# Turning and adding the partial sums of capsule routing in one product with stacked identities

## The chip, the cores and the metric

One core of one Trainium2 chip runs the whole program. The metric is the device time of one execution in microseconds (us); for the kernel before it is 13064.68 us, the median of three runs (13056.39 to 13068.2).

## The reference

The input is 16 images of 32 channels and 64x64 pixels. Two layers are added to it. The first, the only one that the change touches, is capsule routing over 3x3 patches: 4 input capsules of 8 channels vote for 4 output capsules of 8 channels, and three rounds weigh the votes.

```python
priors = jnp.einsum('nfdhwij,ofijud->nhwofiju', patches, weight)
logits = jnp.zeros_like(priors)
for r in range(3):
    probs = softmax(logits, axis=-3)
    out = jnp.sum(probs * priors, axis=-2, keepdims=True)
    if r != 2:
        out = squash(out)
        logits = logits + jnp.sum(priors * out, axis=-1, keepdims=True)
out = squash(out)
```

`squash(s)` is s·n²/((1+n²)·sqrt(n²+1e-12)) with n the length of a capsule's vector. The second layer is chunked attention with an MLP over the same patches, folded back. All of it is float32 at the borders.

## The kernel before, in words

The program has five phases with barriers between them: a norm, routing, a norm, attention, the fold. Only the routing phase changes.

**Tiling.** A pass handles half an image; there are 32 passes. A half has four lanes of 512 pixels. All 128 partitions hold 4 input capsules x 32 channels. A lane meets 9 taps (the 3x3 positions), and each tap is one tile of 128x512.

**Slots.** The work of a pass is laid out in 16 slots, in a loop whose body holds two passes. Slots 0 to 3 and 8 to 11 are voting slots (lane 0 to 3, rounds 0 and 1), slots 4 to 7 and 12 to 15 are summing slots. In a slot TensorE (`make`) writes nine tap tiles into four PSUM tiles `r_pg` in turn: in a voting slot with two bfloat16 products a tap (L582, L583), in a summing slot with four float32 transposes of 128x128 a tap (L587, out of `r_spread`). Each tile is multiplied by a shifted window of the image: seven taps on VectorE (L849), two on GpSimd (L524), for which ScalarE first copies the tile to SBUF (L790). TensorE then reduces the nine product tiles over channels (`batch`): L629 and L632 are taps in eights of instructions, L621 and L618 are tap 8. In a summing slot the result `r_ps` holds four partial sums of the lane: each 32 partitions of the 128 hold the sum over some of the taps.

**The order inside a slot** is written out by hand. TensorE: the first three taps; a light part C; tap 8 and then taps 4 to 7 of the slot before (this last group of eight products is called the mark of a slot below); a second light part C; four more taps; the light part A; the last two taps; taps 0 to 3 of this slot. VectorE: the product of the first tap; light part B; four products; light part A, with the last two products filled in between its steps. A tile of `r_pg` is written again only when the product four taps back has been read, and a batch waits for its products.

**Lights.** Beside the tap work each slot has small steps on a lane that was finished before. A squash light goes as follows. ScalarE copies `r_ps` to `r_sums` (L733). Part A on TensorE turns it with four float32 transposes of 128x128 (L663) into the PSUM tile `r_pt`: pixels are then on partitions, and the 512 columns are four blocks of pixels x four partial sums x 32 channels. VectorE adds the four partial sums with one tensor_reduce (L866), writing 128 columns to `r_cap`, then squares (L871), sums to lengths (L873), and computes 1+n² (L875) and its reciprocal (L878, L881); ScalarE computes the inverse root (L745, L748). Part B on VectorE scales (L908, L913) and in round 1 adds to the vote (L921). ScalarE and GpSimd split the vote in three bfloat16 parts (L762, L763, L547, L765, L549), and part C on TensorE turns them back (L668), or turns the output (L674). The squash lights of round 1 have their part A in slots 5 to 8, those of round 2 in slots 13 to 15 and slot 0 of the next pass. Slot 13 has also the round-0 light of the next pass, whose sums come from a uniform product over the image (L647) and which VectorE takes with a copy (L863). Slots 1 to 4 and 9 to 12 have softmax lights (L680, L888, L893).

All of the small constants are loaded by SyncE at the start of the phase, and TensorE and VectorE wait for them on the semaphore `fixed`.

Of the kernel before, what the change touches and what calls it, by code (L numbers as in the profile page):

```python
# [17 lines left out]
ALU = mybir.AluOpType  # L18
ACT = mybir.ActivationFunctionType
EXP_LN = "natural_log_exp_and_others"  # L20
AX_X = mybir.AxisListType.X

C = 32
# [10 lines left out]
LANES = 4  # L34
CHUNK = 512
CROWS = CHUNK // IMG
BLK = CHUNK // 128
# [291 lines left out]
def routing_phase(nc, ctx, sems, halves, routed, w_sum, w_vote, w_uniform, consts):  # L329
# [5 lines left out]
    def sb(n, shape, dt=F32):  # L335
        return ctx.enter_context(nc.sbuf_tensor(f"r_{n}", shape, dt))
# [12 lines left out]
    ident = sb("ident", [128, 128])  # L349
    ident_b = sb("ident_b", [128, 128], BF16)  # L350
    pick = sb("pick", [128, 2, C])
    eps = sb("eps", [128, 1])
    prod = sb("prod", [128, TAPS, CHUNK])

# [136 lines left out]

    @block.sync
    def _(sp):
        for to, src in ((ws[:, :, :], w_sum), (wu[:, :, :], w_uniform), (ident[:, :], consts["ident"]), (pick[:, :, :], consts["pick"])):
            sp.dma_start(to, src).then_inc(fixed, 16)
        for k in range(4):
            sp.dma_start(wv_f[C * k:C * k + C, :], w_vote).then_inc(fixed, 16)
        with sp.Fori(0, passes // 2) as i:
            for h in range(2):
                n = 2 * i + h  # L500

                sp.wait_ge(products.sem, products.at(n, -n_dve * SLOTS))
                sp.wait_ge(pooled.sem, pooled.at(n, -len(POOLED) * SLOTS))
                for k in range(CAPS):
                    to = win[C * k:C * k + C, h, :, :].rearrange("p a b -> p (a b)")
                    sp.dma_start(to, halves[n, :, :]).then_inc(loaded[h].sem, 16)
                image = halves[n, :, :].rearrange("c (a b) -> c a b", b=PAD)
                for j in range(3):
                    to = wsh[C * j:C * j + C, h, :].rearrange("p (a b) -> p a b", b=IMG)
                    sp.dma_start(to, image[:, :, j:j + IMG]).then_inc(loaded[h].sem, 16)  # L510
# [43 lines left out]
    @block.tensor  # L554
    def _(pe):
        pe.sem_inc(reduced.sem, reduced.base)
        pe.wait_ge(fixed, 16 * 8)
        pe.wait_ge(prepared, 1)

        def make(n, s, pos):  # L560
# [90 lines left out]
        def light(p, x, which):  # L651
            d, kind, r, lane, part = x
            n = p.to(d).n

            before = reader_before(x, which)
            if before:
                free, k = before
                pe.wait_ge(free.sem, free.at(p.n, k))
            if kind == "squash" and part == "A":
                own = sums[:, 1 + lane % 2 if r else 0, :]  # L660
                pe.wait_ge(sum_copied[r].sem, sum_copied[r].at(n, lane + 1))
                for b in range(BLK):
                    last = pe.transpose(pt[:, 128 * b:128 * b + 128], own[:, 128 * b:128 * b + 128], ident[:, :])  # L663
                last.then_inc(sum_turned[r].sem, 1)
            elif kind == "squash" and r < 2:
                pe.wait_ge(part2[r].sem, part2[r].at(n, lane + 1 if r else 1))
                for b in range(BLK):
                    last = pe.transpose(pt_b[:, 128 * b:128 * b + 128],  # L668
                                        parts[:, lane, b, :, :].rearrange("p a b -> p (a b)"), ident_b[:, :])
                last.then_inc(parts_turned[r].sem, 1)  # L670
            elif kind == "squash":
                pe.wait_ge(squashed[2].sem, squashed[2].at(n, lane + 1))
                for b in range(BLK):
                    last = pe.transpose(pt[0:C, 128 * b:128 * b + 128], sq[:, 1, lane, C * b:C * b + C], ident[:, :])  # L674
                last.then_inc(out_turned.sem, 1)
            else:
                pe.wait_ge(logit_copied[r].sem, logit_copied[r].at(n, lane + 1))
                pe.wait_ge(logit9_copied[r].sem, logit9_copied[r].at(n, lane + 1))
                for b in range(BLK):
                    pe.transpose(pt[:, 128 * b:128 * b + 128], logit[:, lane % 2, 128 * b:128 * b + 128], ident[:, :])  # L680
                last = pe.transpose(pl9[:, 0:128], logit9[:, lane % 2, :], ident[:, :])
                last.then_inc(logit_turned[r].sem, 1)
# [139 lines left out]
    def _(dve):  # L822
# [8 lines left out]
            dve.wait_ge(chain, step[0])  # L831

        dve.wait_ge(fixed, 16 * 8)
        link(nc.vector.tensor_copy(wv_0[:, :], wv_f[:, :]))
        link(nc.vector.tensor_tensor(wv_r[:, :], wv_f[:, :], wv_0[:, :], ALU.subtract))
        link(nc.vector.tensor_copy(wv_1[:, :], wv_r[:, :]))
# [16 lines left out]
        def light_a(n, kind, r, lane, fill):  # L854

            k = lane + 1
            if kind == "squash":
                own = int(r > 0)
                c, s2, nm, fc = (tile[:, own, lanes_of(r, lane), :].rearrange("p l x -> p (l x)")
                                 for tile in (cap, sq, norm, fac))  # L860
                dve.wait_ge(sum_turned[r].sem, sum_turned[r].at(n, k))
                if r == 0:
                    last = nc.vector.tensor_copy(cap[:, 0, :, :].rearrange("p l (b c) -> p l b c", c=C),  # L863
                                                 pt[:, :].rearrange("p (b l c) -> p l b c", b=BLK, c=C))
                else:
                    last = nc.vector.tensor_reduce(c.rearrange("p (b c) -> p b c", c=C),  # L866
                                                   pt[:, :].rearrange("p (b g c) -> p b c g", b=BLK, c=C), AX_X, ALU.add)
                last.then_inc(summed[r].sem, 1)
                fill()
                dve.wait_ge(summed[r].sem, summed[r].at(n, k))  # L870
                nc.vector.tensor_tensor(s2, c, c, ALU.mult).then_inc(squared[r].sem, 1)  # L871
                dve.wait_ge(squared[r].sem, squared[r].at(n, k))
                nc.vector.tensor_reduce(nm, s2.rearrange("p (k u) -> p k u", u=CLEN), AX_X, ALU.add).then_inc(normed[r].sem, 1)  # L873
                dve.wait_ge(normed[r].sem, normed[r].at(n, k))
                nc.vector.tensor_scalar(fc, nm, 1.0, None, ALU.add).then_inc(plus1[r].sem, 1)  # L875
                fill()
                dve.wait_ge(plus1[r].sem, plus1[r].at(n, k))
                nc.vector.reciprocal(fc, fc).then_inc(recip[r].sem, 1)  # L878
                fill()
                dve.wait_ge(recip[r].sem, recip[r].at(n, k))  # L880
                nc.vector.tensor_tensor(fc, fc, nm, ALU.mult).then_inc(ratio[r].sem, 1)  # L881
                return
            dve.wait_ge(logit_turned[r].sem, logit_turned[r].at(n, k))

            pieces = ((pt[:, :].rearrange("p (k x) -> p k x", x=16), 0, 32),
                      (pl9[:, 0:128].rearrange("p (k x) -> p k x", x=C)[:, :, 0:16], 32, 36))
            for src, a, b in pieces:
                nc.vector.tensor_reduce(top[:, lane, 4 * a:4 * b].rearrange("p (k f) -> p k f", f=CAPS),  # L888
                                        src.rearrange("p k (o f) -> p k f o", o=CAPS), AX_X, ALU.max).then_inc(maxed[r].sem, 1)
            fill()  # L890
            dve.wait_ge(maxed[r].sem, maxed[r].at(n, 2 * k))
            for src, a, b in pieces:
                last = nc.vector.tensor_tensor(  # L893
                    low[:, lane, 16 * a:16 * b].rearrange("p (k o f) -> p k o f", o=CAPS, f=CAPS),
                    src.rearrange("p k (o f) -> p k o f", o=CAPS),
                    over_capsules(top[:, lane, 4 * a:4 * b], b - a), ALU.subtract)
            last.then_inc(shifted[r].sem, 1)
# [921 lines left out]
        finish(Pass(samples - 1, 1, samples // 2 - 1), 1)  # L1819

def program(nc, x, w_sum, w_vote, w_uniform, w_r, w_qkv, w_p, w_1, b_1, w_2, ident, pick, pairs,
            sample, count, sel, result):

    batch = x.shape[0]
# [13 lines left out]
    def phase(body, *args):  # L1839

        sems = []
        with ExitStack() as ctx:
            body(nc, ctx, sems, *args)
        nc.clear_and_free_semaphores(sems)
        nc.all_engine_barrier()

    phase(norm_phase, "n1", rows, None, dict(pairs=pairs), first)
    phase(routing_phase, first, routed, w_sum, w_vote, w_uniform, dict(ident=ident, pick=pick))
    phase(norm_phase, "n2", rows, routed, dict(pairs=pairs, sample=sample, count=count), second, layered, total)
    phase(attention_phase, second, layered, mixed, moments, w_r, w_qkv, w_p, dict(ident=ident))  # L1850
    phase(fold_phase, mixed, moments, total, result.rearrange("b c h w -> (b c) (h w)"), w_1, w_2, b_1,
# [3 lines left out]
def lay_out(inputs):  # L1855
# [14 lines left out]
    for p in range(128):  # L1870
# [8 lines left out]
        w_qkv=inputs["L1_conv_Wqkv"].T, w_p=w_p.reshape(QUADS, 128, 3, 3 * C),  # L1879
        w_1=inputs["L1_conv_W1"].reshape(HID, C, 3, 3).transpose(3, 1, 2, 0).reshape(3 * C, 3, HID),  # L1880
        b_1=inputs["L1_conv_b1"].reshape(HID, 1), w_2=w_2.reshape(3 * C, 3, 3 * C),
        ident=np.eye(128, dtype=f), pick=pick,
        pairs=np.kron(np.eye(64, dtype=f), np.full((2, 2), 0.5, f)),
        sample=np.kron(np.eye(4, dtype=f), np.full((C, C), 1 / (PIX * DIM), f)),
        count=np.outer(times, times).reshape(1, PIX),
# [19 lines left out]
```

## Time and profile before

| | |
|---|---|
| Median of three runs | 13064.68 us (13056.39 to 13068.2) |
| Profiled execution | 13060.79 us, span 13059.0 us |
| Mean granted TensorE clock | 0.982 |
| TensorE matmul busy | 12449.1 us, 95% |
| TensorE weight load busy | 5276.3 us, 40% |
| VectorE busy | 9722.8 us, 74% |
| ScalarE busy | 7866.5 us, 60% |
| GpSimd busy | 2684.0 us, 21% |

The span is that of the core from its first to its last instruction. Matmuls are pipelined, and their ends are modelled, so a busy share of TensorE overstates how full the engine is: the distance between the starts of successive instructions tells more. PE is TensorE's matmul, PEld its weight load, DVE VectorE, ACT ScalarE, POOL GpSimd. Idle time in brackets is that of the engine in front of the row, with what ended it.

### The profile page before, as it was taken

The page shows a single profiled execution, that of the slowest core. Times are in us where ns is not written, and L with a number is a line of the kernel's source. Part 1 is how long each engine was busy: PE and PEld are TensorE (multiplying, and loading weights), DVE is VectorE, ACT ScalarE, POOL GpSimd, SP SyncE. Part 2 cuts the span into 40 slices and gives each one's busy share as a digit, 9 for nine tenths or more (in the row PEclk, how much of TensorE's full clock was granted, in tenths as well). Part 3 has the DMA queues.
Part 4 walks back from the last instruction along what each step waited for, and adds up shares of the span by engine and source line. Part 5 has one row for each costly group of instructions (what it writes and reads, how often), then busy time and mean ns, then how long its engine had stood idle before and what let it go on. Part 6 is the DMA issues. An engine that isn't in the chain of part 4 may idle for free. (4 is left out here: it accounts for less than half of the span.)

```text
span 13059.0 us, 258656 instructions
## 1 busy us (share of the span) xinstructions
PE 12449.1 (95%) x76092; PEld 5276.3 (40%) x76348; DVE 9722.8 (74%) x18034; ACT 7866.5 (60%) x14774; POOL 2684.0 (21%) x2692
## 2 busy tenths in 40 slices
PE   6999999999996499999999999999999999999899
PEld 3555555555553133333333333333333333333233
DVE  7888888888887577777777777777777777777311
ACT  4666666666665166666666666666666666666411
POOL 3454444544443000000000000000000000000143
PEclk9999999999998699999999999999999999999999
DMA  3101011010112523223222232332322323223255
GB/s 77 22 15 22 17 20 22 15 22 15 22 21 55 132 64 75 66 66 73 66 70 69 67 72 66 73 70 64 75 66 67 72 66 71 68 69 72 64 124 109
DMA packets 853225, 771.45 MB, mean 59 GB/s; under 512 B 587076, under 2 KB 621348, under 8 KB 840740
## 3 DMA queue, kind: packets, MB, share of 16 engines
q1 hardware_dynamic: 850468, 747.29, 25.4%
q8 instruction: 703, 11.52, 0.4%
q10 hardware_dynamic: 1536, 8.39, 0.3%
q14 instruction: 518, 4.24, 0.1%
HBM read 510.50 MB, written 244.96 MB: 58 GB/s over the span
## 5 line engine op out<-in xcount | busy, mean ns | idle before, releaser
L1503 DVE TENSOR_REDUCE a_big<-a_mp 128x1 f32<-128x512 f32 x8192 | 5222.3, 685 | 1816.0 <-PE a_mp L1337 1797.7
L1423 ACT ACTIVATE a_ex<-a_sc 128x512 f32<-128x512 f32 x8192 | 4426.4, 601 | 1937.6 <-PE a_sc L1325 1932.6
L1337 PE MATMUL a_mp<-a_ks,a_qs 108*128 108x512 bf16 x8192 | 3131.1, 383 | 39.9 <-DMA a_ks<-qk_parts 25.1
L1325 PE MATMUL a_sc<-a_qs,a_ks 111*128 111x512 bf16 x8192 | 3124.5, 383 | 6.8 <-ACT a_ex L1423 4.5
L849 DVE TENSOR_TENSOR r_prod<-r_pg,r_win 128x512 f32<-128x512 f32 x3584 | 2319.4, 683 | 416.5 <-PE r_pg L583 227.9
L1351 PE MATMUL a_po<-a_ex,a_va 128*32 128x512 f32 x16384 | 2183.0, 605 | 2.1 <-ACT a_oc L1429 0.7
L1239 POOL TENSOR_TENSOR a_pieces<-a_left,a_pieces 128x512 bf16<-128x512 f32 x256 | 295.5, 1154 | 7319.5 <-ACT a_pieces L1409 7319.5
L1325 PEld LDWEIGHTS a_sc<-a_qs,a_ks 111*128 111x128 bf16 x8192 | 794.9, 97 | 2477.6 <-ACT a_ex L1423 1767.0
L524 POOL TENSOR_TENSOR r_prod<-r_temp,r_win 128x512 f32<-128x512 f32 x1024 | 1214.7, 1207 | 1298.3 <-PE r_pl L632 568.3
L587 PE MATMUL r_pg<-r_ident,r_spread 128*128 128x128 f32 x9216 | 1196.7, 278 | 113.3 <-DVE r_prod L849 94.5
L587 PEld LDWEIGHTS r_pg<-r_ident,r_spread 128*128 128x128 f32 x9216 | 1004.9, 142 | 573.0 <-DVE r_prod L849 275.1
L1337 PEld LDWEIGHTS a_mp<-a_ks,a_qs 108*128 108x128 bf16 x8192 | 803.2, 98 | 913.6 <-DVE a_big L1503 237.7
L807 ACT ACTIVATE r_spread<-r_low 128x2048 f32<-128x2048 f32 x512 | 952.1, 1916 | 0.0
L582 PE MATMUL r_pg<-r_stack,r_wv 96*128 96x512 bf16 x2304 | 882.3, 383 | 28.4 <-DVE r_prod L849 10.1
L583 PE MATMUL r_pg<-r_stack,r_wv 128*128 128x512 bf16 x2048 | 778.4, 380 | 0.0
L1269 PE MATMUL a_pm<-a_zw,a_wc 96*128 96x512 f32 x1536 | 711.1, 599 | 15.1 <-DVE a_left L1473 13.4
L1351 PEld LDWEIGHTS a_po<-a_ex,a_va 128*32 128x32 f32 x16384 | 322.5, 107 | 824.7 <-ACT a_ex L1423 702.6
L629 PE MATMUL r_ps<-r_prod,r_ws 128*32 128x512 f32 x4096 | 553.3, 613 | 22.8 <-DVE r_prod L849 15.6
L1808 DVE TENSOR_TENSOR f_u<-f_pw,f_three 96x512 f32<-96x512 f32 x128 | 87.9, 687 | 651.4 <-PE f_pw L1677 650.1
L790 ACT COPY r_temp<-r_pg 128x512 f32<-128x512 f32 x1024 | 544.1, 583 | 20.4 <-ACT r_out_t L775 20.4
L632 PE MATMUL r_pl<-r_prod,r_pick 128*32 128x512 f32 x4096 | 541.1, 600 | 5.3 <-DVE r_prod L849 0.3
L1723 ACT ACTIVATE f_hidden<-f_ph,f_coef 72x512 f32<-72x512 f32 x128 | 99.0, 773 | 652.2 <-PE f_ph L1667 652.2
(192 smaller groups left out, 11795.2 us busy)
## 6 DMA issues: line engine op xcount, KB each, us to landing
a_qs<-qk_parts SPq DMA_DIRECT2D x768, 144.0 KB
a_ks<-qk_parts SPq DMA_DIRECT2D x768, 144.0 KB
qk_parts<-a_pieces SPq DMA_DIRECT2D x128, 768.0 KB, 5.0
f_t<-mixed SPq DMA_DIRECT2D x48, 1536.0 KB, 16.7
a_tw<-second SPq DMA_DIRECT2D x512, 128.0 KB, 3.1
mixed<-a_t SPq DMA_DIRECT2D x256, 256.0 KB, 2.1
r_win<-first SPq DMA_DIRECT2D x128, 280.5 KB, 5.2
a_zw<-layered SPq DMA_DIRECT2D x192, 144.0 KB, 12.2
```

The costliest lines, as they stand in the source:

```text
L524: nc.gpsimd.tensor_tensor(prod[:, g, :].rearrange("p (a b) -> p a b", b=IMG), temp[:, rank, :].rearrange("p (a b) -> p a b", b=IMG), tap_a ...
L582: pe.matmul(bank[:, :], wv_0[0:96, w], stack[0:96, lane, :], start=True, stop=False)
L583: last = pe.matmul(bank[:, :], wv_12[:, w], stack[:, lane, :], start=False, stop=True)
L587: last = pe.transpose(bank[:, 128 * b:128 * b + 128], spread[:, lane, 16 * kk:16 * kk + 16, :].rearrange("p a b -> p (a b)"), ident[:, :])
L807: nc.scalar.activation(to[:, :, half, :], src[:, :, half].unsqueeze(3).to_broadcast([128, BLK, 64, CLEN]), ACT.Exp).then_inc(prob[r].sem, 1)
L849: nc.vector.tensor_tensor(prod[:, g, :].rearrange("p (a b) -> p a b", b=IMG), pg[use % RINGS][:, :].rearrange("p (a b) -> p a b", b=IMG), ...
L1269: last = pe.matmul(pm[:, :], wc[:, i, 128 * (k % WIDE):128 * (k % WIDE) + 128], zw[:, own.h, first:first + CHUNK], start=i == 0, stop=i == 2)
L1325: pe.matmul(sc[k % BANKS][:, :], ks[0:KROWS + NPART, p.h, head, 128 * kb:128 * kb + 128], qs[0:KROWS + NPART, p.h, head, CHUNK * qb:CHUNK ...
L1337: pe.matmul(mp[k % BANKS][:, :], qs[0:KROWS, p.h, head, 128 * q:128 * q + 128], ks[0:KROWS, p.h, head, CHUNK * half:CHUNK * half + CHUNK], ...
L1351: last = pe.matmul(po[32 * x:32 * x + 32, :], va[:, p.h, kb, QUAD * quad + x, :], ex[:, (QUAD * t + x) % RING, :], start=kb == 0, stop=kb ...
L1423: nc.scalar.activation(ex[:, k % RING, :], sc[k % BANKS][:, :], ACT.Exp, scale=scale).then_inc(exped.sem, 1)
L1503: nc.vector.tensor_reduce(big[:, x % 2, k // 2:k // 2 + 1], mp[k % BANKS][:, :], AX_X, ALU.max).then_inc(maxed.sem, 1)
```

## The change

In rounds 1 and 2 the four transposes of part A become four products. Each takes the same 128x128 block of `r_sums` as its stationary operand, and as its moving operand, in place of the 128x128 identity, a new constant `gather` of 128x32: four 32x32 identities on top of one another. One such product turns the block and adds its four partial sums, so the result has 32 columns for a block and 128 for the lane. VectorE's tensor_reduce over 512 columns becomes a tensor_copy of 128 columns from PSUM to SBUF. Round 0 is unchanged. The constant is one more load at the start of the phase, so the waits on `fixed` go from 8 to 9 loads.

```diff
+    gather = sb("gather", [128, C])
 ...
-        for to, src in ((ws[:, :, :], w_sum), (wu[:, :, :], w_uniform), (ident[:, :], consts["ident"]), (pick[:, :, :], consts["pick"])):
+        for to, src in ((ws[:, :, :], w_sum), (wu[:, :, :], w_uniform), (ident[:, :], consts["ident"]), (pick[:, :, :], consts["pick"]), (gather[:, :], consts["gather"])):
 ...
-        pe.wait_ge(fixed, 16 * 8)
+        pe.wait_ge(fixed, 16 * 9)
 ...
                 for b in range(BLK):
-                    last = pe.transpose(pt[:, 128 * b:128 * b + 128], own[:, 128 * b:128 * b + 128], ident[:, :])
+                    if r == 0:
+                        last = pe.transpose(pt[:, 128 * b:128 * b + 128], own[:, 128 * b:128 * b + 128], ident[:, :])
+                    else:
+                        last = pe.matmul(pt[:, C * b:C * b + C], own[:, 128 * b:128 * b + 128], gather[:, :],
+                                         start=True, stop=True)
 ...
-        dve.wait_ge(fixed, 16 * 8)
+        dve.wait_ge(fixed, 16 * 9)
 ...
-                    last = nc.vector.tensor_reduce(c.rearrange("p (b c) -> p b c", c=C),
-                                                   pt[:, :].rearrange("p (b g c) -> p b c g", b=BLK, c=C), AX_X, ALU.add)
+                    last = nc.vector.tensor_copy(c, pt[:, 0:BLK * C])
 ...
+        ident=np.eye(128, dtype=f), pick=pick, gather=np.tile(np.eye(C, dtype=f), (LANES, 1)),
```

## Rows read from the trace of the kernel before

**Rows 1.** Busy by stretch (length, PE, PEld, DVE, ACT, POOL, clock, DMA): routing; rows 4.

```profile
326.00:3600.00 3274.00, 3128.63 (x24793) 1668.18 (x24992) 2853.01 (x5705) 2130.08 (x3683) 1635.45 (x1708) 0.99 0.11 19
...
12285.00:12287.00 2.00, 1.22 (x8) 1.12 (x8) 0.53 (x3) 0.00 (x0) 0.00 (x0) 0.50 1.01 221
```

**Rows 2.** Groups of instructions, VectorE: busy us, mean ns, idle before, releaser.

```profile
L866 DVE TENSOR_REDUCE r_cap<-r_pt 128x128 f32<-128x512 f32 x256 | 174.1, 680 | 68.6 <-PE r_pt L663 68.6
...
L893 DVE TENSOR_TENSOR r_low<-r_pl,r_top 128x64 f32<-128x64 f32 x256 | 54.9, 214 | 0.0
...
L863 DVE COPY r_cap<-r_pt 128x512 f32<-128x512 f32 x32 | 22.0, 687 | 10.8 <-PE r_pt L663 10.8
```

**Rows 3.** Groups of instructions, TensorE: products and weight loads, float32.

```profile
L1305 PEld LDWEIGHTS a_pm<-a_on,a_wp 128*128 128x128 f32 x1024 | 194.2, 190 | 165.5 <-issue 124.5 <-DVE a_t L1496 2.4 <-DVE a_on L1485 1.1
L663 PE MATMUL r_pt<-r_ident,r_sums 128*128 128x128 f32 x1152 | 176.1, 275 | 2.0 <-ACT r_sums L733 1.2 <-ACT r_sums L730 0.8
...
L1310 PEld LDWEIGHTS a_pm<-a_on,a_wp 128*32 128x32 f32 x1024 | 26.9, 110 | 40.3 <-DVE a_t L1496 28.8 <-issue 0.7
```

**Rows 4.** Timeline, TensorE: start us, us, runs of one float32 product, two places.

```profile
5083.44 2.37 PE L1282 MATMUL a_pm<-a_wc,a_zw 96*128 96x144 f32 x18
...
12285.49 0.80 PEld L1655 LDWEIGHTS f_px<-f_ones,f_w 96*72 96x72 f32 x6 [22.94 <-issue]
```

**Rows 5.** Timeline, VectorE, slots 6 to 10 of one pass: start us, us.

```profile
1562.40 0.69 DVE L849 TENSOR_TENSOR r_prod<-r_pg,r_win 128x512 f32<-128x512 f32 x1
...
1564.60 1.16 DVE L921 TENSOR_TENSOR r_vote<-r_vote,r_sq 128x128 f32<-128x128 f32 x1
...
1580.17 2.48 DVE L849 TENSOR_TENSOR r_prod<-r_pg,r_win 128x512 f32<-128x512 f32 x4 [1.10 <-PE r_pg L583]
...
1587.07 2.48 DVE L849 TENSOR_TENSOR r_prod<-r_pg,r_win 128x512 f32<-128x512 f32 x4 [0.97 <-PE r_pg L583]
```

**Rows 6.** Timeline, TensorE, the same pass, slots 5 to 10; L629, L632: marks.

```profile
1539.82 1.04 PE L629 MATMUL r_ps<-r_prod,r_ws 128*32 128x512 f32 x8
...
1546.45 0.43 PE L621 MATMUL r_ps<-r_prod,r_ws 128*32 128x128 f32 x8
1546.69 1.04 PE L629 MATMUL r_ps<-r_prod,r_ws 128*32 128x512 f32 x8
...
1555.46 1.06 PE L629 MATMUL r_ps<-r_prod,r_ws 128*32 128x512 f32 x8
...
1558.26 0.60 PE L663 MATMUL r_pt<-r_ident,r_sums 128*128 128x128 f32 x4
...
1562.26 0.38 PE L668 MATMUL r_pt<-r_ident_b,r_parts 128*128 128x128 bf16 x4
1562.57 0.42 PE L621 MATMUL r_ps<-r_prod,r_ws 128*32 128x128 f32 x8
1563.14 1.07 PE L629 MATMUL r_ps<-r_prod,r_ws 128*32 128x512 f32 x8
...
1578.53 1.06 PE L632 MATMUL r_pl<-r_prod,r_pick 128*32 128x512 f32 x8
```

**Rows 7.** Timeline, GpSimd, the same pass: start us, us, idle before.

```profile
1553.62 0.43 POOL L549 TENSOR_TENSOR r_parts<-r_rest,r_parts 128x128 bf16<-128x128 f32 x1 [0.41 <-ACT r_parts L765]
...
1564.32 2.48 POOL L524 TENSOR_TENSOR r_prod<-r_temp,r_win 128x512 f32<-128x512 f32 x2 [3.96 <-PE r_ps L629]
```

**Rows 8.** Timeline, TensorE, slot 14: start us, us, idle before.

```profile
1616.09 1.25 PE L587 MATMUL r_pg<-r_ident,r_spread 128*128 128x128 f32 x8 [2.08 <-DVE r_prod L849]
...
1621.35 1.06 PE L629 MATMUL r_ps<-r_prod,r_ws 128*32 128x512 f32 x8 [0.75 <-DVE r_prod L849]
```

**Rows 9.** Timeline, VectorE, slots 14 to 0, two passes: start us, us, idle before.

```profile
1496.60 2.48 DVE L849 TENSOR_TENSOR r_prod<-r_pg,r_win 128x512 f32<-128x512 f32 x4 [0.91 <-PE r_pg L587]
...
1619.58 1.12 DVE L875 TENSOR_SCALAR r_fac<-r_norm 128x16 f32<-128x16 f32 x1
...
1630.67 2.48 DVE L849 TENSOR_TENSOR r_prod<-r_pg,r_win 128x512 f32<-128x512 f32 x4 [0.84 <-PE r_pg L583]
```

More of the change, by code:

```diff
@@ L1819, in _, with program @@
         finish(Pass(samples - 1, 1, samples // 2 - 1), 1)
-def program(nc, x, w_sum, w_vote, w_uniform, w_r, w_qkv, w_p, w_1, b_1, w_2, ident, pick, pairs,
+def program(nc, x, w_sum, w_vote, w_uniform, w_r, w_qkv, w_p, w_1, b_1, w_2, ident, pick, gather, pairs,
             sample, count, sel, result):
@@ L1847, in program @@
     phase(norm_phase, "n1", rows, None, dict(pairs=pairs), first)
-    phase(routing_phase, first, routed, w_sum, w_vote, w_uniform, dict(ident=ident, pick=pick))
+    phase(routing_phase, first, routed, w_sum, w_vote, w_uniform, dict(ident=ident, pick=pick, gather=gather))
     phase(norm_phase, "n2", rows, routed, dict(pairs=pairs, sample=sample, count=count), second, layered, total)
@@ L1881, in lay_out @@
         b_1=inputs["L1_conv_b1"].reshape(HID, 1), w_2=w_2.reshape(3 * C, 3, 3 * C),
-        ident=np.eye(128, dtype=f), pick=pick,
+        ident=np.eye(128, dtype=f), pick=pick, gather=np.tile(np.eye(C, dtype=f), (LANES, 1)),
         pairs=np.kron(np.eye(64, dtype=f), np.full((2, 2), 0.5, f)),
```

## The prediction

> **What bounds the kernel now.** I read the busy time by stretch first, because the change lies in routing alone. In its steady part of 3274 us TensorE's matmuls are busy for 3129 us and VectorE for 2853 us, at a granted clock of 0.99 [rows 1]. Neither is idle enough to be ignored, so the groups of instructions give the prices of the pieces, and the timeline of one pass shows which engine ends each slot. Marks are what to follow there: the eight products with which TensorE closes the slot before. Where VectorE starts its four products straight behind its own work, VectorE sets the slot; where there is idle time in front of them that TensorE ends, TensorE does.
>
> Two kinds of squash slot come out. In slots 6 to 8 VectorE runs without a gap. The last product that the mark of slot 7 needs ends at 1562.40 + 0.69 = 1563.09, and the mark comes at 1563.14 [rows 5, 6]: TensorE waited for VectorE. The marks stand 1563.14 − 1555.46 = 7.68 us apart. In the slots around them TensorE sets the pace: 0.97 and 1.10 us of idle before VectorE's four products in slots 10 and 11 [rows 5], 0.91 us in slot 15 and 0.84 us in slot 0 [rows 9].
>
> **The change, part by part.** *VectorE* loses a reduction of 680 ns, 256 times: 8 in each of 32 passes [rows 2]. The copy of 128 columns from PSUM doesn't stand in the trace. The nearest rows are the copy of 512 columns at 687 ns and an operation of 64 columns from PSUM at 214 ns; they give (687 − 214)/448 = 1.06 ns a column and 214 + 64 × 1.06 = 282 ns, between 214 and 687. I take 280, so 0.40 us less a light, 102 us in all if VectorE were the bound everywhere.
>
> *TensorE* had four transposes. A run of four lasts 0.60 us and one lasts 0.275, so they start (0.60 − 0.275)/3 = 0.108 us apart [rows 3, 6], and the four take 0.43 us. A float32 product that is no transpose is two instructions with a weight load each: a mark is four calls, one a tap, and its rows show x8 [rows 6]. So the new light has eight loads of 128 columns and eight products of 32. The price is in the load. A load of 128 columns lasts 190 ns, one of 32 lasts 110 [rows 3]: 0.83 ns a column, 107 ns for 128 at the higher clock level. Where products have one column only, loads set the pace: six of 72 columns take 0.80 us with about 0.24 for the first, at a granted clock of 0.50 [rows 1, 4], so 0.112 apart, 0.056 at full clock, 0.78 ns a column, 100 ns for 128. The loads run beside products: 18 products of 144 columns, with loads of 128, take 2.37 us [rows 4], at most 2.37/18 = 0.132 apart and about 0.123 with the last one's 0.28 us taken as 275 ns like L663's [rows 3], and 144 columns alone are 0.120 at the same 0.83 ns. So eight take 8 × 0.107 = 0.853, and about 0.03 more because the last product of 32 columns (27 ns at 0.120/144 a column) no longer covers the load behind it: 0.88 us. TensorE has D = 0.45 us more a light. The lower end of the price is 8 × 0.027 = 0.22 us, loads free, D = −0.21; the upper end is eight whole loads of 190 ns, 1.52 us, D = 1.08. I stay with the loads' pace, which the two places of rows 4 carry.
>
> The rule that speaks against the change is in the Trainium skill, "TensorE: Matmul & The Clock Gate", Part 3, The mechanism: a weight load overlaps running products only where the row groups differ, and here they are all the same. By it load and product add up, 8 × 0.134 = 1.07 us and D = 0.63; the 0.123 us above speaks against it, since load and stream would be 0.107 + 0.120 there.
>
> *Slots 5 to 8 (round 1).* I carry the marks forward. Slot 5 to slot 6 was 1546.69 − 1539.82 = 6.87 with TensorE never waiting [rows 6]; it becomes 7.32, mark at 1547.14. A slot with a part C costs 0.31 more (1562.26 to 1562.57), so TensorE alone would need 6.87 + 0.31 + 0.45 = 7.63 for the next. But part C waits for the split vote, done at 1553.62 + 0.43 = 1554.05, which is 7.36 behind the old mark and hangs on ScalarE's long exponentials, started by that mark [rows 7]. With 0.05 for the signal and 0.31 + 0.24 from part C to the mark [rows 6] the next mark is at 1547.14 + 7.36 + 0.60 = 1555.10 instead of 1555.46. Then 7.63 gives 1562.73 instead of 1563.14. Slot 8 is a voting slot; a softmax voting slot with a part C, paced by TensorE, takes 1587.07 − 1580.17 = 6.90 [rows 5]; a transpose fewer (0.11) and D make 7.24, mark at 1569.97. Slot 9 is then TensorE's at 6.90: 1576.87 instead of 1578.53. The gain is 1.66 us a pass. It rests on VectorE no longer being the bound. Its slot was 7.68 and has 0.40 less, 7.28, below 7.63. What it held beyond that was a stall: L921, 1.16 us, stands beside GpSimd's product, which started at 1564.32, released by the mark [rows 5, 7]. If VectorE gets there before the mark releases GpSimd, that stall goes too. VectorE is late no more; next is TensorE itself.
>
> *Slots 13 to 0 (round 2).* In slot 13 the light is waited for by VectorE: its start moves by between D − 0.40 = 0.05 and D; I take 0.23. In slot 14 TensorE idles 2.08 us right behind the light [rows 8], which hides D. There the mark waits 0.75 us for VectorE, and VectorE's L875 has lasted 1.12 us [rows 8, 9]: with 0.40 less it runs before the GpSimd work that holds it. So this mark gains those 0.75 and the 0.18 by which a run like L621 (0.42 to 0.43) outlasts its 0.24 to the mark, less the 0.23: −0.70, in one pass of two. In the other the four products of slot 15 wait for TensorE [0.91, rows 9], nothing is gained, and 0.23 is lost. Slots 15 and 0 are TensorE's: 2 × 0.45 lost. Over two passes −0.70 + 0.23 + 1.80 = 1.33, so 0.66 a pass.
>
> *The new constant* is one more small load in a queue; at most 1 us, once.
>
> Sum: −1.66 + 0.66 = −1.00 a pass, × 32 = −32 us, and with the load −31. From the profiled 13060.79 that is 13030; the profiled execution stands 4 below the median of the runs, so I name 13064.7 − 31.5 = 13033. The sum has a slope: each 0.1 us of D costs 3 × 0.1 in slots 5 to 8 (slot 6 has cover) and as much in the others, 6 × 0.1 × 32 = 19 us. It is even at D = 0.62.
>
> **The rivals.** *A, TensorE pays and VectorE's time isn't wanted.* Loads don't overlap. Slots become longer by D where TensorE is the bound, and from D = 0.78 in slot 6 too. With D = 0.63 the pass has −1.00 + 6 × 0.18 = +0.08, 13068; with D = 1.08 it has −1.00 + 6 × 0.33 + 7 × 0.30 = +3.08, 99 us, 13163. It is slower by more than 26 us from D = 0.75 on. For: the load, 190 ns, is seven times its product. Against: the 0.123 us. Chance 0.10.
>
> *B, no change.* VectorE stays behind in slots 6 to 9, because GpSimd's product, released by the mark, still meets L921, and the two stalls at slots 9 and 14 stay. Then slots 5 to 9 give 0.40 instead of 1.66, slot 14 only 0.40 − 0.23 = 0.17 instead of 0.70, and the pass has −0.40 + (−0.17 + 0.23 + 1.80)/2 = +0.53, 17 us: 13082. With half of the 1.66 it would be +0.10, 13068. For: the collision came in nearly every slot of this kind. Chance 0.30.
>
> *C, more than forecast.* D is hidden in slots 15 and 0 too (TensorE's order has waits there that the view credits to nothing), or ScalarE's chain in slot 6 is shorter. Then −1.66 − (0.70 − 0.23)/2 = −1.90 a pass, 61 us: 13004. For: little. Chance 0.15.
>
> *D, the change doesn't do what it says*: the copy is held up by GpSimd as L921 is and costs as much as the reduction. Against: L863 and L866, which read PSUM, average 687 and 680 ns over all their runs [rows 2]; that holds them to one price. Nothing would be saved, and slots 15 and 0 would cost 0.90 a pass, 29 us: 13094; chance 0.03.
>
> **How the numbers follow.** The forecast has 0.42, with its own range 13015 to 13050. No change can be told here within 0.2%, 26 us, so 13039 is the border of faster. Of the forecast two thirds lie below, 0.28; with a tenth of B and all of C that is 0.28 + 0.03 + 0.15 = 0.46. Slower by more than 26 us (above 13091): most of A, some of B and D, 0.11. Within: 0.43. The range reaches from C's side to B's upper end and a part of A: 12995 to 13088.
>
> **What would show it.** L663 as x8 in a run of about 0.95 us in rounds 1 and 2, loads 0.107 apart at 190 ns each. The copy at 280 ns. Marks of slots 6 to 8 about 7.6 apart, now with idle time of VectorE, L921 near 290 ns instead of 1160. Slots 15 and 0 longer by 0.45. The forecast is wrong if the run of eight lasts over 1.2 us, if L921 keeps 1.16 us, or if the marks keep 7.68.

## The result, and the profile after

| | before | after |
|---|---|---|
| Median of 20 runs | 13064.01 us (13056.23 to 13068.75) | 13082.74 us (13070.99 to 13097.76) |
| Profiled execution | 13060.79 us | 13070.99 us |
| Span, mean granted TensorE clock | 13059.0 us, 0.982 | 13069.2 us, 0.980 |

The ratio is 1.0014, with an interval of 1.0008 to 1.0021: the kernel is 19 us slower. That is inside the range of the prediction and within its 0.2%, but the forecast, 31 us faster, had the sign wrong.

The busy times moved as they should. First the page's part 1 of after, then the same stretch of routing as [rows 1] (length, PE, PEld, DVE, ACT, POOL, clock, DMA).

```profile
PE 12518.9 (96%) x77372; PEld 5425.0 (42%) x77372; DVE 9482.7 (73%) x18034; ACT 7854.6 (60%) x14774; POOL 2677.2 (20%) x2692
```

```profile
326.00:3600.00 3274.00, 3175.35 (x25735) 1784.20 (x25724) 2649.85 (x5683) 2112.18 (x3667) 1625.04 (x1703) 0.99 0.11 19
```

VectorE has 240 us less to do, TensorE 70 us more matmul and 149 us more weight load. The groups of after, by shape (busy us, mean ns, idle before, releaser), give the prices:

```profile
L667 PEld LDWEIGHTS r_pt<-r_gather,r_sums 128*128 128x128 f32 x2048 | 253.5, 191 | 36.8 <-issue 26.0 <-ACT r_out_t L780 1.5
L667 PE MATMUL r_pt<-r_gather,r_sums 128*128 128x32 f32 x2048 | 253.0, 267 | 1.2 <-ACT r_sums L738 1.2
L871 DVE COPY r_cap<-r_pt 128x128 f32<-128x128 f32 x256 | 71.6, 280 | 82.2 <-PE r_pt L667 82.2
L925 DVE TENSOR_TENSOR r_vote<-r_vote,r_sq 128x128 f32<-128x128 f32 x128 | 37.3, 292 | 4.4
L879 DVE TENSOR_SCALAR r_fac<-r_norm 128x16 f32<-128x16 f32 x256 | 44.6, 174 | 8.9
L917 DVE TENSOR_TENSOR r_sq<-r_cap,r_fac 128x128 f32<-128x128 f32 x256 | 103.7, 405 | 8.7
```

The copy costs 280 ns, as priced. The vote (L925, before L921) fell from 149.3 us of busy time in the kernel before to 37.3. All of its executions, before and then after (duration ns min/median/max, first and last start):

```profile
L921 DVE TENSOR_TENSOR r_vote<-r_vote,r_sq x128: 1152/1159/1310, 158.1 to 4098.6; 128x128 f32<-128x128 f32 x128
```

```profile
L925 DVE TENSOR_TENSOR r_vote<-r_vote,r_sq x128: 291/292/293, 159.0 to 4106.5; 128x128 f32<-128x128 f32 x128
```

In the kernel before all 128 begin while a GpSimd operation runs, in the kernel after none does. L879 and L917 (before L875 and L913) fell from means of 290 and 548 ns to 174 and 405 in the same way: of L913's 256 executions 68 begin beside a running GpSimd operation and take 1.25 us, and the other 188 take 0.29; of L917's 31 do. So of VectorE's 240 us some 102 are the copies' (256 × 0.40), and nearly all of the rest is time lost beside GpSimd.

TensorE in slots 5 to 10 of a pass (start us, us, runs of one instruction); L630 and L633 are the marks:

```profile
1416.40 1.04 PE L630 MATMUL r_ps<-r_prod,r_ws 128*32 128x512 f32 x8
...
1419.17 0.98 PE L667 MATMUL r_pt<-r_gather,r_sums 128*128 128x32 f32 x8
...
1423.68 1.04 PE L630 MATMUL r_ps<-r_prod,r_ws 128*32 128x512 f32 x8
...
1431.18 0.38 PE L673 MATMUL r_pt<-r_ident_b,r_parts 128*128 128x128 bf16 x4 [0.38 <-POOL r_parts L550]
...
1431.74 1.04 PE L630 MATMUL r_ps<-r_prod,r_ws 128*32 128x512 f32 x8
...
1439.20 1.04 PE L630 MATMUL r_ps<-r_prod,r_ws 128*32 128x512 f32 x8
...
1446.58 1.04 PE L633 MATMUL r_pl<-r_prod,r_pick 128*32 128x512 f32 x8
...
1453.69 1.04 PE L633 MATMUL r_pl<-r_prod,r_pick 128*32 128x512 f32 x8
```

The marks are 7.28, 8.06, 7.46, 7.38 and 7.11 apart, where [rows 6] has 6.87, 8.77, 7.68 and, for the last two together, 15.39. VectorE and GpSimd in the same pass:

```profile
1432.06 0.29 DVE L925 TENSOR_TENSOR r_vote<-r_vote,r_sq 128x128 f32<-128x128 f32 x1
1433.40 2.48 DVE L854 TENSOR_TENSOR r_prod<-r_pg,r_win 128x512 f32<-128x512 f32 x4 [1.05 <-PE r_pg L588]
...
1440.82 2.48 DVE L854 TENSOR_TENSOR r_prod<-r_pg,r_win 128x512 f32<-128x512 f32 x4 [0.47 <-PE r_pg L584]
```

```profile
1432.89 2.35 POOL L525 TENSOR_TENSOR r_prod<-r_temp,r_win 128x512 f32<-128x512 f32 x2 [1.85 <-PE r_ps L630]
...
1440.35 2.33 POOL L525 TENSOR_TENSOR r_prod<-r_temp,r_win 128x512 f32<-128x512 f32 x2 [3.89 <-PE r_ps L630]
```

VectorE's vote ends at 1432.35, and only then, at 1432.89, does GpSimd start, released by the mark. VectorE now waits for TensorE (1.05 and 0.47 us in brackets); in the pass of [rows 5] its products of slots 6 to 8 follow its other work without a gap.

Below, a table of marks says how much later or earlier each mark follows the one before than it does in the kernel before, as means in us over the passes of the loop. The row of a slot is the time from its mark to the next one. The forecast's column has its own steps.

| Mark of slot | forecast | after |
|---|---|---|
| 5 to 6 | +0.45 | +0.41 |
| 6 to 7 | −0.81 | −0.71 |
| 7 to 8, to 9, to 10 | −0.05, −1.25 for the other two | −0.21, −0.30, −0.61 |
| slot 13, with its light | +0.23 | +0.25 |
| slot 14, in the pass of [rows 8] | −0.93 (−0.70 with slot 13's) | +0.25 |
| slot 14, in the other pass | 0 | +0.09 |
| slots 15 and 0, inside the loop's body | +0.45, +0.45 | +0.39, +0.37 |
| slot 15, at the end of the loop's body | +0.45 | +2.15 |
| slot 0 behind it | +0.45 | +0.02 |

Slots 5 to 9 (round 1) gained 1.42 us a pass, near the forecast's 1.66. Two lines are far off: slot 14, and the place where TensorE's loop ends, once in two passes. At the loop's end the trace of after reads so (TensorE's timeline):

```profile
1498.88 0.98 PE L667 MATMUL r_pt<-r_gather,r_sums 128*128 128x32 f32 x8
1499.69 1.07 PE L588 MATMUL r_pg<-r_ident,r_spread 128*128 128x128 f32 x8
1500.70 1.06 PE L630 MATMUL r_ps<-r_prod,r_ws 128*32 128x512 f32 x8
1503.79 0.51 PE L583 MATMUL r_pg<-r_stack,r_wv 96*128 96x512 bf16 x1 [2.03 <-issue]
1504.09 0.63 PE L584 MATMUL r_pg<-r_stack,r_wv 128*128 128x512 bf16 x1
```

TensorE is idle for 2.03 us, and no engine ends the wait: "issue" stands for time in which it waited for nothing that the profile shows. The loop's own line at this place (duration ns min/median/max, first and last start):

```profile
L317 PEldq COMPARE_BRANCH  x1: 3592/3592/3592, 1499.8 to 1499.8; - x1
```

The branch back to the loop's start took 3.6 us. TensorE worked off what was already queued and then had nothing to run. In that same stretch the DMA view shows one packet, of the queue that carries instructions:

```profile
DMA  0000000000080000000000000000000000000000
...
DMA packets 1, 0.02 MB, mean 5 GB/s; under 512 B 0, under 2 KB 0, under 8 KB 0
...
q8 instruction: 1, 0.02, 2.1%
```

It stands in the twelfth of 40 slices of 1499.80 to 1503.40, so about 1.0 us after the branch began, and the branch ends 2.6 us behind it. Over all 15 executions of the branch (the last one isn't taken, 80 ns), before, then after:

```profile
L317 PEldq COMPARE_BRANCH  x15: 80/836/2447, 488.0 to 4024.6; - x15
```

```profile
L317 PEldq COMPARE_BRANCH  x15: 80/3333/3793, 485.4 to 4032.7; - x15
```

The 14 taken ones have a mean of 1.30 us before and 3.32 us after. The same branch takes 44 to 90 ns on the other engines in both. The Trainium skill, "Runtime: NRT & Kernel Launch", section Instruction fetch mechanics, describes this: instructions are streamed in order in 16 KiB blocks, "Branching breaks sequential prefetch", and a taken branch whose target isn't in the window stalls until the target is fetched. The trace agrees in so far as a packet of 0.02 MB of the instruction queue stands inside the branch and TensorE runs dry; in these two kernels the taken branch lasts 0.35 to 3.8 us.

### The profile page after: what moved, and what is told of

It is laid out like the page before. It is cut to its first block and busy times, and to the rows that moved or that the text cites. A ratio compares the mean times of both kernels' runs of the same rounds, so it can differ in the third digit from the quotient of the medians.

```text
span 13069.2 us, 260961 instructions
## 1 busy us (share of the span) xinstructions
PE 12518.9 (96%) x77372; PEld 5425.0 (42%) x77372; DVE 9482.7 (73%) x18034; ACT 7854.6 (60%) x14774; POOL 2677.2 (20%) x2692
## 5 line engine op out<-in xcount | busy, mean ns | idle before, releaser
L584 PE MATMUL r_pg<-r_stack,r_wv 128*128 128x512 bf16 x2304 | 877.3, 381 | 0.0
L630 PE MATMUL r_ps<-r_prod,r_ws 128*32 128x512 f32 x4096 | 560.6, 620 | 1.0 <-DVE r_prod L854 1.0
L633 PE MATMUL r_pl<-r_prod,r_pick 128*32 128x512 f32 x4096 | 539.4, 598 | 0.0
```

What stands on the lines that cost most here:

```text
L584: last = pe.matmul(bank[:, :], wv_12[:, w], stack[:, lane, :], start=False, stop=True)
```

## The experiments

Each was timed in three or five rounds against the kernel before on the same chip; the chips differ between groups of experiments, so each time is compared with the kernel before beside it. After each stands the ratio with its interval. The marks are again means against the kernel before. The theory at the start was that the parts do what was foretold and that what is lost comes at the loop's end and in slot 14; rivals were that VectorE's saving or TensorE's cost was mis-sized.

**One part at a time.** The kernel before with the copy alone (e1: it copies 128 columns of the transposes' result and leaves the sum of the four parts out), and the kernel after with the reduction of 512 columns kept (e2: it adds columns that the product didn't write).

```diff
 # e1, on the kernel before
-  last = nc.vector.tensor_reduce(c..., pt[:, :]..., AX_X, ALU.add)
+  last = nc.vector.tensor_copy(c, pt[:, 0:BLK * C])
 # e2, on the kernel after: the reverse
```

> The four transposes stay; VectorE copies the first 128 columns instead of reducing 512, so one partial sum of one block is taken where the sum of four belongs. TensorE's instructions are those of before, to the last one. Theory 1 (the slots behave as forecast, and what made the change slower is TensorE's taken branch at the end of the loop, 0.84 us in the median before and 3.33 after): the branch stays near 0.8 us, the marks of slots 6 to 9 come 0.5 to 0.8 us earlier each, slot 14 gains too, together about 3 us a pass: 12970 to 12990. Theory 2 (VectorE's time is not wanted, TensorE is the bound everywhere): within 25 us of before.

e1: 13001.97 us (12998.52 to 13007.31), 0.9958 (0.9945 to 0.9972), 56 us faster, and less than the 12970 to 12990 expected. The vote keeps its stall (in 122 of 128 executions):

```profile
L866 DVE COPY r_cap<-r_pt 128x128 f32<-128x128 f32 x256 | 71.8, 280 | 68.6 <-PE r_pt L663 68.6
...
L920 DVE TENSOR_TENSOR r_vote<-r_vote,r_sq 128x128 f32<-128x128 f32 x128 | 143.3, 1119 | 4.4
```

Round 1 gains 1.21 us a pass, by 0.30, 0.44, 0.40 and 0.07 in slots 6 to 9: VectorE is the bound, and three of its slots are shorter by about its 0.40. The branch, expected near 0.8, has a median of 1.92 us, though every instruction of TensorE is that of the kernel before.

> The eight products are there, and VectorE still runs its reduction over 512 columns, of which 384 are old, so what it adds up is not the sum. Theory 1: +0.41 us in the mark of slot 5, little in slots 6 to 9 where VectorE sets the pace, +0.4 in slots 15 and 0, +0.45 or more in slot 13, about 1.5 us a pass = 48 us, and on top the branch at 3.3 us, some 18 us more: 13125 to 13135. Theory 2 (no effect of the branch): the same without the 18, about 13110, and the branch near 0.8 us.

e2: 13079.86 us (13072.61 to 13085.86), 1.0017 (1.0008 to 1.0026). A miss, and the most telling one: VectorE still pays 683 ns a light, and yet round 1 has the marks of the kernel after to 0.01 us (+0.41, −0.71, −0.21, −0.30, −0.60), and the vote's stall is gone:

```profile
L871 DVE TENSOR_REDUCE r_cap<-r_pt 128x128 f32<-128x512 f32 x256 | 174.7, 683 | 82.1 <-PE r_pt L667 82.1
...
L926 DVE TENSOR_TENSOR r_vote<-r_vote,r_sq 128x128 f32<-128x128 f32 x128 | 37.4, 292 | 4.4
```

So in round 1 VectorE's 0.40 us is not what was gained. TensorE being later was. In the whole kernel, too, e2 and the kernel after can't be told apart (1.0017 and 1.0014 of the kernel before).

**That, by itself.** The kernel before with the four transposes of round 1 done twice: pure extra work, nothing of the change (f1).

```diff
-  for b in range(BLK):
+  for b in [*range(BLK)] * (2 if r == 1 else 1):
```

> The kernel before, with one addition: in round 1 TensorE does the four transposes of part A twice over, the second time onto the first. It is work for nothing, 0.43 us and 8 instructions a light; VectorE's reduction stays. Theory 1 (round 1 gains because a later TensorE releases GpSimd's product later, so that VectorE's addition to the vote no longer meets it, and the shorter VectorE operation has no part in it): the marks of slots 5 to 9 are those of the changed kernel (+0.41, -0.71, -0.21, -0.30, -0.61 us), the kernel is faster by about 39 us, 13020 to 13030. Theory 2 (round 1 gains by VectorE's 0.40 us): +0.41 in slot 5 and no gain behind it, 13065 to 13080.

13020.73 us (13016.28 to 13025.2), 0.9972 (0.9961 to 0.9982): useless work makes the kernel 36 us faster. Marks of round 1: +0.44, −0.72, −0.19, −0.23, −0.60. The branch is short here as well (0.35 us), but at the loop's end that changes little: slot 15 is 0.50 shorter there and slot 0 behind it 0.62 longer. The reduction is whole, the vote free, and the light's row is now a run of eight, as in after:

```profile
L866 DVE TENSOR_REDUCE r_cap<-r_pt 128x128 f32<-128x512 f32 x256 | 174.0, 680 | 68.7 <-PE r_pt L663 68.7
...
L921 DVE TENSOR_TENSOR r_vote<-r_vote,r_sq 128x128 f32<-128x128 f32 x128 | 37.3, 292 | 4.4
```

```profile
1421.42 1.04 PE L663 MATMUL r_pt<-r_ident,r_sums 128*128 128x128 f32 x8
```

**The two rounds apart.** The kernel after with the change in round 1 alone (e3) and in round 2 alone (e4); the condition stands in both places, TensorE's and VectorE's.

```diff
-  if r == 0:
+  if r != 1:      # e4: if r != 2
```

> Only round 1 (slots 5 to 8) has the new product and copy, round 2 stays as before. By the marks of the changed kernel round 1 gains 1.45 us a pass, 46 us. TensorE's loop body is longer by 64 instructions instead of 128. Theory 1, if the branch grows with the length of the body: between 0 and 18 us of the gain is lost, 13018 to 13036, with the branch between 0.8 and 3.3 us in the median. If the branch depends on the length in steps it is at one of the two ends. Theory 2 (the changed kernel's loss is the light's own price, in both rounds): 13070 to 13075, half of the loss.

> Only round 2 (slots 13 to 15 and slot 0) has the new product and copy. By the marks of the changed kernel, without the wait at the loop's end, it loses about 1.05 us a pass, 34 us. Theory 1: that and the branch, 13098 to 13116. Theory 2 (half of the loss each): 13070 to 13075. The sum of this one's and the round-1 kernel's differences should give the changed kernel's +19 us if the rounds don't meet; a rest between them is the branch's.

e3: 13019.43 us (13012.63 to 13022.4), 0.9970 (0.9959 to 0.9981). e4: 13059.5 us (13054.7 to 13065.69), 1.0002 (0.9993 to 1.0011). Apart they are worth −39 and +1 us, together +19: 56 us are in neither part. e3 came as expected in time; e4 is 39 us below its lower forecast of 13098 and 11 below the other theory's 13070. The ratios of e3 and f1 can't be told apart: in round 1 the change is worth what doing the transposes twice is worth. In both e3 and e4 the branch takes 0.35 us, shorter than in the kernel before; here e3:

```profile
L317 PEldq COMPARE_BRANCH  x15: 80/349/391, 486.1 to 3984.5; - x15
```

e4 shows slot 14 in two passes. The same two runs, TensorE:

```profile
2123.26 1.97 PE L588 MATMUL r_pg<-r_ident,r_spread 128*128 128x128 f32 x8 [1.71 <-DVE r_prod L854]
2125.16 1.68 PE L630 MATMUL r_ps<-r_prod,r_ws 128*32 128x512 f32 x8
...
2376.02 1.25 PE L588 MATMUL r_pg<-r_ident,r_spread 128*128 128x128 f32 x8 [1.71 <-DVE r_prod L854]
2377.22 1.06 PE L630 MATMUL r_ps<-r_prod,r_ws 128*32 128x512 f32 x8
```

```profile
2123.00:2127.00 4.00, 3.74 (x18) 2.00 (x19) 3.93 (x10) 3.22 (x7) 1.49 (x2) 0.57 0.00 0
2376.00:2380.00 4.00, 3.98 (x32) 2.64 (x32) 3.93 (x10) 3.03 (x7) 1.72 (x2) 1.00 0.00 0
```

After the same idle time of 1.71 us the clock is granted at 0.57 on average over 4 us in one pass, which is the lower level (1.2 of 2.4 GHz) in most of it, and at 1.00 in the other: the two runs take 3.58 us instead of 2.26. So slot 14 gains where the clock holds and gains nothing where it falls. By the marks, of what e3 and e4 together lack of the kernel after's loss, 2.4 us in two passes is at the loop's end and 1.2 is in slot 14.

**The loop's end without the change.** The kernel before with 32 small bfloat16 transposes in slot 14 of one lane, where TensorE idles 2 us. With their weight loads the loop's body grows by 128 instructions, as it does with the change (f2).

```diff
+  if r == 2 and lane == 1:
+      for _ in range(32):
+          pe.transpose(pt_b[:, 0:128], ident_b[:, :], ident_b[:, :])
   pe.wait_ge(sum_copied[r].sem, sum_copied[r].at(n, lane + 1))
```

> The kernel before, with 32 bfloat16 transposes of an identity (64 instructions) in front of part A in slot 14 of each pass, where TensorE idles 2.1 us: the loop body has 128 instructions more, as in the changed kernel, and nothing of the change. Theory 1: the branch at the end of the loop rises from 1.3 us in the mean to about 3.3, slot 15 to 0 is longer by 1.5 us in one pass of two, 13075 to 13090. Theory 2 (the branch's wait comes from what the change does in time, not from the length of the body): branch as before, 13050 to 13065.

13085.39 us (13077.65 to 13090.9), 1.0021 (1.0011 to 1.003), 26 us slower. The mark at the loop's end comes 2.43 us later, where 1.5 was expected. The branch:

```profile
L317 PEldq COMPARE_BRANCH  x15: 80/3533/3774, 487.5 to 4047.8; - x15
```

**The change, with its code moved.** The kernel after, with N waits on a semaphore that has its value already, ahead of routing's first product. They do nothing but move TensorE's later code; the trace shows N/2 instructions more.

```diff
   pe.wait_ge(fixed, 16 * 9)
   pe.wait_ge(prepared, 1)
+  for _ in range(N):          # N = 64, 128, 192, 256
+      pe.wait_ge(fixed, 16 * 9)
```

> The changed kernel, with 64 waits more in TensorE's program in front of its first product of routing, each on what has already come, at a place where TensorE waits for data anyway. The loop itself is the same, only 64 instructions further back in memory. Theory 1 (the taken branch of TensorE's loop waits for the 16 KB piece of its program that holds the loop's start, and when that is fetched hangs on where the loop's ends lie in such pieces): the branch leaves 3.3 us, towards 0.35 or up to the 2.4 of before, and with 0.35 the kernel is faster than the changed one by 25 to 55 us, because the idle times that lower TensorE's clock go as well: 13030 to 13060. Theory 2 (the wait is the price of a longer loop, wherever it lies): 3.3 us, 13083.

> As the kernel with 64 waits, with 128. A piece of 16 KB holds 256 instructions of 64 bytes if they are of one length, so 64, 128 and 192 are quarters of a turn. Theory 1: the three differ from one another, at least one has the branch near 0.35 us and at least one above 2 us. Theory 2: all three have 3.3 us and 13083.

> As the kernel with 64 waits, with 192. Theory 1: see there; the one of the three with the shortest branch runs at 13030 to 13060. Theory 2: 3.3 us and 13083.

> The changed kernel with 256 waits more (the trace counted 32 instructions for 64 waits, so 128 here) in front of TensorE's first product of routing. So far the branch was 3.32, 2.76, 2.00 and 1.19 us in the mean with 0, 32, 64 and 96 instructions. Theory 1 (the place of the loop's ends in the pieces that are fetched): the row goes on to 0.35 to 0.6 us, the attention loop's branch back to about 0.36, and the kernel runs at 13035 to 13050; TensorE's low-clock stretches in slot 14 stay, so it doesn't reach the forecast. Theory 2 (chance): the branch is anywhere between 0.35 and 3.5.

| N | time, us | ratio (interval) | branch, median ns |
|---|---|---|---|
| 64 | 13118.43 | 1.0045 (1.0029 to 1.006) | 2770 |
| 128 | 13051.52 | 0.9996 (0.9986 to 1.0005) | 2235 |
| 192 | 13046.77 | 0.9991 (0.9981 to 1.0) | 752 |
| 256 | 13033.73 (13032.13 to 13042.92) | 0.9981 (0.9972 to 0.9991) | 349 |

```profile
L317 PEldq COMPARE_BRANCH  x15: 80/349/387, 489.4 to 4001.7; - x15
```

The last has all the work of the kernel after and 256 idle waits, and is 25 us faster than the kernel before beside it, where after is 19 slower. With 64, 128 and 192 waits the branch had been expected near 0.35 us at least once; only N = 256 has it. N = 64 was a miss with a reason: its routing is faster than after's, but the code of the attention phase moved too, and that phase's loop, 30 executions, now pays. Before, then N = 64:

```profile
L986 PEldq COMPARE_BRANCH  x30: 88/357/393, 5020.1 to 12051.1; - x30
```

```profile
L992 PEldq COMPARE_BRANCH  x30: 87/3008/3692, 5022.5 to 12116.1; - x30
```

From the first to the last branch this phase lasts 7093.6 us instead of 7031.0, and nothing of the change is in it.

**Which lights are worth it.** Round 1 and one lane of round 2 (f4, the condition `r == 1 or r == 2 and lane == 1`), or two (g3, lanes 1 and 3).

> The new product and copy in round 1 and in lanes 1 and 3 of round 2 (slots 14 and 0); lanes 0 and 2 (slots 13 and 15) as before. The body is longer by 96 instructions. Slot 14 had 10.80 us instead of 11.60 where the clock held, slot 0 lost 0.37 and won back a collision of VectorE with GpSimd in slot 0 that costs 1.24 us in the next mark. Theory 1: with a short branch -1.45 - 0.6 - 0.4 us a pass, 12980 to 13000; with a branch of 2 to 3 us some 20 more, 13000 to 13020. Theory 2 (round 2's light costs what it costs in each slot): no better than round 1 alone, 13020 or more.

> The new product and copy in round 1 and in lane 1 of round 2 (slot 14), body longer by 80 instructions. Theory 1: round 1 alone (-39 us) and the gain of slot 14, 0.8 us a pass where the clock holds, about 0.4 in the mean, 13 us: 13000 to 13015 with a short branch. The collision in slot 0 stays, so it is behind the kernel with lanes 1 and 3 unless that one's branch is longer. Theory 2: 13020.

g3: 13013.28 us (13006.9 to 13018.3), 0.9964 (0.995 to 0.9978); it missed its 13000. The collision in slot 0 that it was to win back stays: the mark behind the loop's end comes 0.56 us later. Where the branch is short, VectorE's light in slot 0 meets GpSimd's product, and the slot takes 8.69 us instead of 7.45 (kernel before), 1.24 more. f4: 13003.53 us (13002.2 to 13012.02), 0.9960 (0.9946 to 0.9973), 55 us faster than the kernel before. It has the lowest median of those that compute the whole, but its interval overlaps those of g3, e3 and f1, so that the added lane pays is not shown. Its branches are short as well (mean 0.35 us), which must be counted to it: the same work at another address need not give this.

## Why the prediction was wrong

*Prices.* They held: copy 280 ns, weight loads 191 ns; the eight products occupy TensorE for 0.81 us (1498.88 to 1499.69 above) for a forecast 0.88, and D, forecast at 0.45, shows as +0.41 in slot 5. Rival A is dead: the eight are 0.10 us apart, where load and product in turn would need 0.134, so the loads overlap, as the 0.123 us of [rows 4] said. Rival D is dead by the copy's 280 ns. Rival B names 13082 us, which is the measured median, and that is chance: in B L921 keeps its stall and slots 5 to 9 give 0.40 us, and here the stall went and they gave 1.42.

*Slots 5 to 9.* −1.42 us a pass instead of −1.66, and L921 lost its 0.87 us. The size came near, in part by luck: the reason given, "It rests on VectorE no longer being the bound", through its 0.40 us, is refuted by e2 and f1. The order of two events decides: the mark releases GpSimd's product, and if VectorE's vote comes first, it takes 0.29 us instead of 1.16. The prediction names this only as a further chance. TensorE's 0.4 us of lateness delays GpSimd enough. VectorE's saving alone (e1) keeps the collision and gains 1.21 in another way. The two gains don't add; they are for the same time.

In the step from slot 6 to 7 one term stood in no row: 0.05 us for the signal from GpSimd to part C. Here part C (L673 at 1431.18) starts 0.15 us after GpSimd's operation ends, and that 0.10 is what lies between −0.81 and −0.71.

*Slot 13*: +0.25 for 0.23, which was a choice between 0.05 and 0.45. *Slots 15 and 0*: +0.39 and +0.37 for 0.45 each, away from the loop's end.

*Slot 14*: forecast −0.93 in one pass of two. A gain of this size is there where the clock holds: the slot takes 10.79 us instead of 11.60, and in the other pass, where nothing was to be gained, also 10.79 instead of 11.59. But the clock fell in this slot in 23 of the loop's 30 passes, against 14 in the kernel before, and then the slot takes 12.3 us (12.1 before); the means are +0.25 and +0.09. [Rows 8] are of a pass where it held. The working took the clock for given; the mean over the steady part doesn't show the falls, 0.99 in both kernels. Why it falls more often in after is not shown.

*The sum.* The step that failed is "Sum: −1.66 + 0.66 = −1.00 a pass": it counts the lights and nothing else. Missing is what 128 more instructions on TensorE do to its loop. Per two passes the forecast had −2.00 us and the marks add to +0.86, a miss of 2.86. The loop's end is 1.70 of it (+2.15 for +0.45), slot 14 is 1.27, round 1 is 0.48; slot 0 behind the loop's end and small terms give 0.59 back. Over the 14 pairs of passes with a taken branch +0.86 is 12 us. From routing's first mark to its last the profiled run of after is 7 us longer, its whole execution 10.2, and the medians differ by 18.7. Within routing the granted clock fell 29 times in after and 14 times in before; six of the 29 are right behind the loop end's idle time, as in the stretch above: L584 at 1504.09 takes 0.63 us instead of 0.38.

With the code moved (N = 256) the loop's end loses nothing (−0.11), the marks add to −1.78, and the kernel is 25 us faster than before for the forecast 31. The profiled run of N = 256 is 34.7 us shorter than that of after from routing's first mark to its last, and that is the loop's end: slots 15 and 0 there take 15.68 us in all 14 iterations, and in after 17.0 to 18.0 in the eight where the clock holds and 19.2 to 19.5 in the six where it falls. So the stall costs about 1.7 us each time, and the fall behind it about 2 more. Slot 14 has 23 falls in both.

That the stall at the loop's end is what turned the sign was shown from three sides: f2 has it without the change, N = 256 has the change without it, and e3 and e4 have the change's parts without it.

## What to carry to other kernels

When a change adds or removes instructions inside a loop's body, read that engine's branch at the loop's end as well as the work; where it is in the microseconds, move the code by some waits ahead of the loop, or change the body's size, before judging the change, and look at the later loops too. Where a slot's time depends on which of two engines comes first to a shared path, try each part of a change alone, and plain delay as well: the gain may belong to the order and not to the saving. Then keep the change only where it pays (here round 1; the lane of round 2 beside it isn't shown to add anything).

## What the runs showed of the hardware

- A taken branch at the end of TensorE's loop took 0.34 to 3.9 us, on the other engines 44 to 90 ns. Where it lasted over 0.4 us it ended 2.3 to 2.9 us after the start of the last packet of TensorE's instruction queue. The engine's queue covers the first part: of 3.59 us it idled 2.03.
- Eight products of 32 columns with float32 loads of 128 columns take 0.98 us, hardly less than eight transposes of 128 columns, 1.04, though a quarter of the columns streams.
- A VectorE addition of 128x128 float32 on SBUF that began while a GpSimd operation ran took 1.16 us (all 128 in the kernel before), and 0.29 us where none ran (all 128 in the kernel after).
- After the same idle time of 1.71 us in the same slot the clock fell in one pass and held in another. With 32 small transposes put into that slot (f2) it never fell there, and fell at the loop's end instead, in seven of 14 iterations.
